# Folding the setup of a four-layer transformer kernel into its first mixture-of-experts block, and moving table and bias loads behind the first slots' loads

## The reference

```python
xn = layernorm(x)                                  # 2048 tokens x 128
logits = xn @ gate_w.T                             # 2048 x 8
probs = softmax(logits); expert = argmax(probs)
rank = position of the token among those of its expert
keep = rank < 320                                  # capacity, ceil(1.25 * 2048 / 8)
slot[expert, rank] = xn[token]                     # kept tokens only
out[expert] = relu(slot[expert] @ w1[expert] + b1) @ w2[expert] + b2
x = x + 0.5 * probs[token, expert] * keep * out[expert, rank]
```

## Time and profile before

| | |
|---|---|
| time, median of 3 runs | 1650.69 us (1649.7 to 1653.43) |
| the profiled execution: its own time / its span | 1644.4 us / 1642.7 us |
| busy over the span: PE, DVE, ACT, POOL | 73%, 51%, 38%, 31% |
| first scatter / first slots' load / first matmul on slots in `moe0_0` | 26.0 / 49.8 / 52.8 us |
| the same last two in `moe0_1` | 409.4 / 415.5 us |

### The profile page before, as it was taken

How to read it: one execution, slowest core, us unless ns; L and a number is a source line. 1 busy time by engine, 2 the same in 40 slices (tenths; PEclk the granted TensorE clock), 3 DMA queues, 4 the chain that set the end, 5 groups by cost and what they waited for, 6 DMA issues and landing times. The chain is left out here.

```text
span 1642.7 us, 24447 instructions
## 1 busy us (share of the span) xinstructions
PE 1207.2 (73%) x8681; PEld 692.9 (42%) x8689; DVE 841.6 (51%) x2201; ACT 616.7 (38%) x1253; POOL 509.0 (31%) x567
## 2 busy tenths in 40 slices
PE   2664899994877858999995975671773888797294
PEld 2442555552565525556553642430551122222173
DVE  5015656642034557667634567773016889982102
ACT  1221445452322224656552123230333477674041
POOL 5452022112230056667200012136462121202543
PEclk9985999997897978999997988775895599998597
DMA  9432422103521026655507200002323221200334
GB/s 199 114 89 68 101 70 64 43 19 110 137 68 34 1 63 195 183 163 169 156 2 110 43 7 0 1 1 92 97 88 105 68 68 34 79 14 10 89 111 121
DMA packets 146336, 130.83 MB, mean 80 GB/s; under 512 B 19343, under 2 KB 129827, under 8 KB 146224
## 3 DMA queue, kind: packets, MB, share of 16 engines
q1 hardware_dynamic: 128480, 108.81, 24.4%
q10 hardware_dynamic: 11088, 8.70, 2.3%
q0 software_dynamic: 6656, 11.88, 2.2%
HBM read 81.86 MB, written 48.37 MB: 79 GB/s over the span
## 5 line engine op out<-in xcount | busy, mean ns | idle before, releaser
L2150 DVE TENSOR_REDUCE att_maxima<-psum 128x2 f32<-128x1024 f32 (+3 forms) x384 | 355.4, 951 | 163.3 <-PE psum L1814 72.9
L2031 ACT ACTIVATE att_probs<-psum 128x512 f32<-128x512 f32 (+1 forms) x640 | 320.3, 553 | 258.5 <-PE psum L1849 105.9
L102 POOL TENSOR_TENSOR rstd<-var_eps,neg_half 128x4 f32<-128x4 f32 x44 | 45.0, 1022 | 589.0 <-DVE var_eps L93 589.0
L1872 PE MATMUL psum<-att_probs,att_values 128*32 128x512 f32 (+3 forms) x1536 | 166.9, 510 | 2.7 <-ACT att_context_t L2038 2.4
L806 POOL DMA_INDIRECT returned<-moe_out,moe_slot_tokens x112 | 107.8, 963 | 156.0 <-DVE moe_out L767 126.2
L1829 PE MATMUL psum<-att_queries,att_keys 50*128 50x512 bf16 (+3 forms) x512 | 121.3, 353 | 30.8 <-ACT att_probs L2031 24.5
L166 PE MATMUL psum<-ident,normalised_rows 128*128 128x128 f32 x192 | 44.1, 374 | 127.9 <-DVE normalised_rows L111 88.8
L687 ACT ACTIVATE moe_hidden<-psum,moe_b 128x320 f32<-128x320 f32 (+1 forms) x128 | 77.8, 607 | 135.3 <-PE psum L618 134.6
L625 PE MATMUL psum<-moe_w,moe_hidden 128*128 128x128 f32 (+1 forms) x784 | 109.5, 286 | 0.0
L618 PE MATMUL psum<-moe_slot_columns,moe_w 128*128 128x320 f32 (+1 forms) x256 | 106.0, 561 | 2.9 <-ACT moe_slot_columns L682 2.9
L1789 PE MATMUL psum<-att_keys,att_queries 48*128 48x512 bf16 (+3 forms) x512 | 94.5, 377 | 17.0 <-DVE att_maxima L2150 16.9
(11 more groups left out here) (254 smaller groups left out, 2127.3 us busy)
## 6 DMA issues: line engine op xcount, KB each, us to landing
score_terms<-att_parts SPq DMA_DIRECT2D x44, 384.0 KB, 2.9
moe_w<-l_w SPq DMA_DIRECT2D x64, 256.0 KB, 3.0
moe_back<-returned SPq DMA_DIRECT2D x24, 256.0 KB, 4.0
att_queries<-score_terms SPq DMA_DIRECT2D x64, 96.0 KB
att_keys<-score_terms SPq DMA_DIRECT2D x64, 96.0 KB
att_queries<-score_terms SPq DMA_DIRECT2D x16, 384.0 KB, 4.2
att_keys<-score_terms SPq DMA_DIRECT2D x16, 384.0 KB, 5.5
dispatched<-untaken SPq DMA_DIRECT2D x2, 2064.0 KB, 26.7
```

The costliest lines, as they stand in the source:

```text
L1872: mm = nc.tensor.matmul(o_bank[VW * j:VW * (j + 1), first_query[s]:T], values[:, b % 2, s, GH * (G % GROUPS) + j, :], probs[:, G % 2, j, o ...
L2031: nc.scalar.activation(probs[:, G % 2, 2 * p + r, unit_at[u]:unit_at[u] + w], g.psum[:, cols_bank + r, 0:w], ACT.Exp).then_inc(probs_ready, 1)
L2150: ins = nc.vector.tensor_reduce(maxima[:, G % 2, t, 2 * p:2 * p + 2], g.psum[:, rows_bank(k):rows_bank(k) + 2, c0:c0 + w], axis=AX, op=ALU ...
```

## The change

`setup` is gone as a block. A class `Lead` holds its five parts, and `moe0_0` runs each of them at the head of the engine's own function. On the way the work is put in another order: routing is done inside it (`choose` of a batch ahead of `place` of the one before, `count` between the matmuls of the logits, the scatters ahead of POOL's masks), the bias table loads stand behind the write of the marks, and zeroing the returned rows and the attention weights' loads stand behind the loads of the first two experts' slots. For every mixture, ACT's bias-tile loads and its layer-2 weight loads stand behind `copy_columns(0, 0)` and a wait for expert 1's slots, and `scale_bias` stands in front of expert 3 in DVE's loop.

```diff
--- before.py
+++ after.py
...
-def setup(g, beside):
...
-        @block.sync
-        def _(sp):
...
-            beside.load(sp)
-            sp.dma_start(g.gamma_beta[:], g.a["l3_gamma_beta"]).then_inc(small_loaded, 16)
-            sp.wait_ge(made, 2)
-
-            write_untaken(g, sp, (0,))
-
-            zero_returned(g, sp, 0)
-            sp.wait_ge(small_loaded, 16 * 5)
...
+class Lead:
+
+    def __init__(self, g, beside, routing):
...
+        self.rank_bank = g.bank[4:8]
+        self.steps = 0
+
+    def sync(self, sp):
+        g = self.g
+        for b in range(B):
+            sp.dma_start(g.x[:, GROUP * b:GROUP * (b + 1), :],
+                         g.a["x"][b * T:(b + 1) * T, :].rearrange("(i p) d -> p i d", p=P)).then_inc(self.loaded[b], 16)
+        for k, n in enumerate(("l0_gate", "l1_gate", "l2_gate", "l3_gate")):
+            sp.dma_start(g.gates[:, k, :], g.a[n]).then_inc(self.small_loaded, 16)
+        sp.dma_start(g.gamma_beta[:], g.a["l3_gamma_beta"]).then_inc(self.small_loaded, 16)
+        sp.wait_ge(self.made, 2)
+        write_untaken(g, sp, (0,))
+        self.beside.load(sp)
+
+    def tensor(self, pe):
...
+        ln_transpose(g, pe, ln, 0, g.bank[0])
+        ln_transpose(g, pe, ln, 1, g.bank[1])
+        ln_logits(g, pe, ln, 0, g.bank[0])
+        ln_transpose(g, pe, ln, 2, g.bank[2])
+        ln_logits(g, pe, ln, 1, g.bank[1])
+        ln_transpose(g, pe, ln, 3, g.bank[3])
+        pe.wait_ge(self.masked, 4)
+        count(0)
+        ln_logits(g, pe, ln, 2, g.bank[2])
+        count(1)
+        ln_logits(g, pe, ln, 3, g.bank[3])
+        count(2)
+        count(3)
+        self.beside.turn(pe, g.bank[0])
+        pe.wait_ge(self.beside.lined, 1)
+
+    def scalar(self, act):
+        g = self.g
+        act.wait_ge(self.masked, 6)
+        g.nc.scalar.copy(g.xn[:, :, D], g.token[:, 0:TILES]).then_inc(self.numbered, 1)
+        ln_columns_and_logits(g, act, self.ln, range(B), lambda b: g.bank[b])
+        self.beside.copy_lines(act, g.bank[0])
+        self.beside.store_lines(act)
+
+    def vector(self, v):
...
+        ln_rows(g, v, ln, B - 1)
+        v.wait_ge(self.made, 2 + E)
+        for b in range(B + 1):
+            if b < B:
+                v.wait_ge(ln.logits, b + 1)
+                routing.choose(v, 0, b)
+            if b >= 1:
+                routing.place(v, 0, GROUP * (b - 1), GROUP, self.rank_bank[b - 1])
+        self.beside.sum_heads(v)
...
+    def gpsimd(self, pool):
...
+        after(nc.gpsimd.tensor_copy(g.token[:], g.token_i[:]))
+        for b in range(B):
+            ln_rstd(g, pool, self.ln, b)
+        pool.wait_ge(self.numbered, 1)
+        for b in range(B):
+            self.routing.scatter(pool, 0, GROUP * b, GROUP, g.xn)
+
+        after(nc.gpsimd.memset(beside.flips[:], 0.0))
...
+        pool.wait_ge(self.routing.scattered, 16 * TILES)
+        for part, unit in enumerate((RelativeBias.UNIT, 1.0)):
...
         @block.sync
         def _(sp):
-            if prefetch:
+            if lead:
+                lead.sync(sp)
+            elif prefetch:
                 prefetch.load(sp)
...
             for i in range(2):
                 load_slots(i, i)
+            if lead:
+                zero_returned(g, sp, 0)
+                prefetch.load(sp)
             with sp.Fori(0, E // 2 - 1) as k:
...
         @block.scalar
         def _(act):
-            if beside:
-                beside.load_tiles(act)
-            if products:
-                products.load(act)
+            if lead:
+                lead.scalar(act)
...
             copy_columns(0, 0)
+            act.wait_ge(d_loaded[1], 16 * tile_loads)
+            if beside:
+                beside.load_tiles(act)
+            if products:
+                products.load(act)
             with act.Fori(0, E // 2 - 1) as k:
...
-            if follow:
-                follow.scale_bias(v)
             v.wait_ge(small_loaded, 32)
             for e in range(E):
                 i, nth = e % 2, e // 2 + 1
+                if follow and e == 3:
+                    follow.scale_bias(v)
...
                     bias = RelativeBias(g, beside, "bias", bias_kq, bias_qk, flips)
-                    setup(g, bias)
-                    mixture("moe0_0", "l0", first, 0, beside=bias, prefetch=weights, follow=begun)
+                    mixture("moe0_0", "l0", first, 0, beside=bias, prefetch=weights, follow=begun, lead=Lead(g, bias, first))
```

More of the change, by code:

```diff
@@ new lines, in __init__ @@
+        self.g, self.beside, self.routing = g, beside, routing
+        self.loaded = [sem(f"x_loaded{b}") for b in range(B)]
+        self.small_loaded, self.made, self.ident_made = sem("small_loaded"), sem("made"), sem("ident_made")
+        self.masked, self.numbered = sem("masks"), sem("rows_numbered")
+        self.ln = LayerNormSems(sem, gate=g.gates[:, 0, :])
+        self.rank_bank = g.bank[4:8]
[11 more added lines that the diff above has]
+        self.beside.load(sp)
@@ new lines, in tensor @@
+    def tensor(self, pe):
+        g, ln = self.g, self.ln
+        pe.wait_ge(self.ident_made, 2)
+        pe.wait_ge(self.small_loaded, 16 * 5)
+        count = lambda b: self.routing.count(pe, b, self.rank_bank[b])
+        ln_transpose(g, pe, ln, 0, g.bank[0])
[13 more added lines that the diff above has]
+        pe.wait_ge(self.beside.lined, 1)
@@ L499, in moe_capacity @@
 def moe_capacity(g, name, routing, routed, w1, b1, w2, b2, last=False, twice=False, gate=None, beside=None, prefetch=None,
-                 products=None, follow=None):
+                 products=None, follow=None, lead=None):
     nc = g.nc
@@ L544, in moe_capacity @@
         rank_bank = g.bank[2:7]
-        to_route = range(routed, B)
+        to_route = range(B if lead else routed, B)
         h_bank = g.bank[2:6]
```

130 lines of the change are left out of this document (51 added, 79 removed).

## The result

The changed kernel is slower: 1668.37 us median (1663.26 to 1675.71, 4 runs) against 1652.06 (1649.7 to 1656.93, 4 runs) of the kernel before beside it, a ratio of 1.0095 with a 95% interval from 1.0066 to 1.0124. A second set of runs gave 1.0071 (1.0040 to 1.0103). I had forecast 1652.9, hardly any change, with 8 chances in 10 between 1640 and 1661, and had given a slower kernel 0.34.

A forecast was written before the change was run, and what follows sets the result against it. The chain from first scatter through landing and slots to expert 0's output was taken to bound the stage. 16.7 us gained there, given back by ACT's hold and PE's clock, left +1.9 and +0.3: 1652.9 us, 8 in 10 for 1640 to 1661.

The forecast's parts named there:

- The earlier first scatter: Start of `moe0_0`: marks requested at 5.4 land at 18.1, so the first scatter starts at 19.1, 6.9 us earlier.
- The quieter landing: Last scatter lands in 2.2 us, slots need 3.0 to PE: PE has them at 43.6 and, in `moe0_1`, 408.0.
- ACT's hold: Behind the slot-column copy, ACT's own load requests delay the first relu: 13.1 us in `moe0_0`, ACT free at 418.8 in `moe0_1`.
- The clock: PE idles before expert 0's output, so its clock halves for about 5 us, costing 2.5 us in each mixture.
- The sum: Expert 0's output ends 1.9 us later in `moe0_0` and 0.3 in `moe0_1`: 2.2 us slower in all.
- rival three: ACT held as long as before, 18.7 and 15.5 us: 14 us slower, 1665; chance 0.17.
- Rival one: Requests do not hold ACT, or only during PE's `hidden(0)`: the full 16.7 us are kept, 1634; chance 0.08.
- Rival two: Short holds of ACT, 8.3 us in `moe0_0` and 4.5 in `moe0_1`: about 10 us faster, 1641; chance 0.17.
- The break-even: The slow side is decided once ACT comes free later than 56.3 us in `moe0_0` and 418.5 in `moe0_1`.

The follow-up runs named there:

- marks_alone: Changed kernel with one wait added on SP, so the bias tables and what follows are requested only once the marks have landed; ratio 1.0075 to the kernel before.
- before_loads_late: Kernel before with only ACT's bias-tile and layer-2 weight loads moved behind the first copy of slot columns and the wait for expert 1's slots; ratio 1.0089.
- sp_early: Changed kernel with SP's zeros and attention weights requested before the wait on the scatters, right behind the tables; one run, 1668.01 us.
- pe_kept_busy: Changed kernel with 170 unread small matmuls (90 in `moe0_1`) on PE ahead of the first expert's output; ratio 1.0019 to the kernel before.
- spread_marks: `loads_spread` with the wait of `marks_alone` added; ratio 0.9921 to the kernel before.
- loads_halved: Changed kernel with half of ACT's requests left at the hold, half behind the fourth expert's relus, no wait for expert 1's slots; ratio 1.0004 to before.
- loads_spread: Changed kernel with ACT's loads issued three bias or one weight request per expert, none at the hold, no wait for expert 1's slots; ratio 0.9982 to before.

## Why the prediction was wrong

The mechanism was the one forecast; it ended far on the slow side because three terms of it were too small, all in the same direction: the landing of the marks, ACT's hold and the half-speed time of PE. By the steps of the prediction:

- **The earlier first scatter: mis-sized.** Routing was ready at 18.06, as worked out (17.6), and the marks' request went out at 5.38 (5.4). But they landed 15.5 us after it, not 12.7, and the first scatter started at 21.86 instead of 19.1. I had taken the landing from the earlier trace rows, where the tables were ahead of the marks, and left out that tables and expert weights, now behind them, share the queues while the marks are written. `marks_alone` gave 12.4 and 18.89.
- **The quieter landing: right.** The last scatter landed in 2.3 us in both mixtures (2.2 taken), the slots needed 3.3 and 2.9 us to PE (3.0). PE had them at 46.76, that is 43.6 plus the marks' delay; and in `moe0_1` at 418.92, which less the 10.9 us by which the block started late is 408.0, the predicted number.
- **ACT's hold: right in kind, too short.** 15.35 us for 13.1, and 10.5 for 9.3. The failed step is the drain of ACT's own requests: I had 9.8 us for it and 3.3 for SP's zeros and attention weights. `before_loads_late` shows 13.07 for the requests alone (`sp_early` 14.34), which leaves 1 to 2.3 for SP's transfers. That 13.07 equals my 13.1 is luck. The queue was judged about right: from 65.2 us, when ACT came free, some 1.05 MB still went out until 71.3 (estimate from the windows of that profile, 173 GB/s over 65 to 71 us), where I had 1.2. The rate was not. While nothing but the bias loads moved, `before_loads_late` shows 181 GB/s, with the DMA engines busy all the time:

```profile
57.00:65.00 8.00, 0.00 (x0) 0.00 (x0) 0.00 (x0) 0.00 (x0) 0.00 (x0) 0.62 1.23 181
```

  I had taken 233 from 42 to 48 us of the kernel before. At 181 my 1.95 MB need 10.8 us and not 8.4. The kernel before has this rate too, at 30 to 32 us, in the hold of its own requests and beside the scatters:

```profile
30.00:32.00 2.00, 0.00 (x0) 0.00 (x0) 1.70 (x11) 0.00 (x0) 1.63 (x2) 1.00 1.25 179
```

  In `moe0_1` the rate was right (290 GB/s over 427 to 435 us, 278 taken). There the loads got under way late: 132 and 111 GB/s in the two microseconds from 421 on.

- **The clock: right in kind, half its size.** I had the first output half at full speed again after 5 us, 2.5 us in each mixture. It ran at half speed for its whole 7.16 us (3.1 lost), and `hidden(1)` behind it as well (1.3 and 2.0): 4.4 and 5.0. `pe_kept_busy` took 5.4 back in `moe0_1`. `hidden(1)` at half speed was a term that I had put at nothing. The 5 us of the earlier trace rows were read from a row of transposes after a long wait for slots, in which the granted clock had not fallen at all: the first hidden values there ran at half speed (4.61 us, 2.42 later on) with 1.00 granted.

```profile
54.42 4.61 PE L618 MATMUL psum<-moe_slot_columns,moe_w 128*128 128x320 f32 x8 [0.66 <-ACT moe_slot_columns L682]
```

```profile
55.00:58.00 3.00, 3.00 (x7) 1.91 (x6) 0.00 (x0) 1.05 (x2) 0.00 (x0) 1.00 0.22 55
```

  I joined that figure to the falls of the earlier trace rows, which said nothing of how long the way back takes.
- **The sum.** `moe0_0` to the start of `hidden(1)`: +7.9 where +1.9 was forecast; 2.8 marks, 0.3 slots, 2.3 hold, 0.6 clock are the 6.0 between. Another 1.3 came with `hidden(1)`. `moe0_1`: +4.1 for +0.3, of which 1.2 hold and 2.6 clock. So 13.3 instead of 2.2, nearly the figure of rival three (14), but not by its way: there the holds were as long as before, 18.7 and 15.5 us. Its figure came out by chance, from shorter holds, later marks and more time at half speed.
- **Rival one** is refuted by `before_loads_late`: the sentence of the Trainium skill ("DMA: Bandwidth & Descriptors", "Issuing engines are not separate DMA queues") that initiating is usually small beside the transfer does not hold where twelve requests go out at once (15.35 us, while their transfers ended by 70), and does hold for the same requests given out by twos between experts (mostly 0.6 to 0.7 us each, 0.20 us of waiting on PE). **Rival two** (8.3 and 4.5 us) is refuted by the same rows, 13.07 at the least and 10.5.
- The break-even was named rightly: ACT free by 56.3 us. That both forecasts lay 1.9 and 0.3 us past it should have widened the range upwards more than downwards, since the unknowns of the hold (neighbours, size of the requests, clock) could lengthen it more easily than shorten it.

## What to carry to other kernels

In this kernel a DMA request cost its engine little (0.6 to 0.7 us) while few were waiting. A batch of twelve, moved out of a transfer's way, put most of its drain time in front of the next instruction of the engine that asked: 13 to 17 us on ACT, 14.6 on SP. Take the rate of that drain from a stretch in which only these loads move. Give such loads out between pieces of work that leave the issuing engine idle anyway, few at a time, and keep the transfer that gates the stage alone in the queues. And count a wait of PE not by its length but with the matmuls behind it that run at half speed: here 10.5 and 5.7 us of waiting cost 4.4 and 5.0 us more.

## What the runs showed of the hardware

- The granted clock fell after PE had gone to work again. In `spread_marks` PE stopped at 71.06, started at 72.93, and the clock, still 1.00 at 73 to 74 us, read 0.63 in the next microsecond and 0.50 until 84, with PE busy all the time. In `pe_kept_busy` PE stopped at 61.83 and started at 65.06; from 65 on it read 0.62, then 0.50 to 72.
- Matmuls ran at half speed with the clock granted in full. In `loads_halved`, after a wait of 1.27 us, the 24 matmuls of the output took 7.16 us (4.09 at full speed), and the windows give 1.00:

```profile
55.00:61.00 6.00, 6.00 (x21) 4.34 (x22) 0.00 (x0) 1.41 (x4) 0.00 (x0) 1.00 1.25 212
```

  In the profiles of `loads_spread`, where PE went on without that wait, they took 4.09 and 4.46. The first hidden values of the kernel before are the other case, shown above (4.61 us with 1.00 granted). The granted clock of a window is thus not all that sets a matmul's time; what else does, no run here tells.
- SP is held by its requests as ACT is: in `sp_early` one request for attention weights behind the zeros took 7.60 us to issue, the next ones 0.43 each.
- The bias loads, 256 KB each, moved at 181 GB/s with the DMA engines busy all the time (share 1.23), the layer-2 weights, 1 MB each, at 290 (windows of 427 to 435 us of the changed kernel, share 1.05).
